# Eight late steps moved from behind the last slots to among them, and the late additions gathered

## The chip, the cores and the metric

The kernel runs on one core of a Trainium2 chip. The metric is the device time of one execution in microseconds; before the change the median of three runs is 490.42 us (490.4 to 490.5). Engines are named as the profile names them: PE is TensorE (PEld its weight loads), DVE VectorE, ACT ScalarE, POOL GpSimd, SP the engine that only issues DMAs.

## The reference

8192 tokens of width 128 (16 sequences of 512) go through two blocks in float32. The first is an RWKV-like layer: a layer norm, four projections, a scan along the sequence, an output projection, a channel mix. The second is a mixture of experts: each token goes to the best of 16 experts, and every token also passes a shared expert.

```python
logits = hidden @ router_w.T
top_vals, top_idx = jax.lax.top_k(logits, K)          # K = 1, N = 16
routed_in = hidden[None, :, :] * scores.T[:, :, None]
gate, up = jnp.split(jnp.einsum('nth,nhf->ntf', routed_in, gate_up_proj), 2, axis=-1)
routed_out = jnp.einsum('ntf,nfh->nth', up * jax.nn.silu(gate), down_proj)
shared = jax.nn.silu(hidden @ shared_gate_w.T) * (hidden @ shared_up_w.T) @ shared_down_w.T
return (shared + routed_out.sum(axis=0)).reshape(b, s, h)
```

Each token's row of the output is its input of this block, plus its one expert's product, plus the shared expert's.

## The kernel before

The kernel has three stages, written out by hand: each engine has a program of its own, and semaphores tie them.

**Rounds** (up to about 345 us of the trace) work on 16 tiles of 512 tokens: the first block, the router, and a part of the shared expert. Each round scatters its tokens' rows, sorted by expert, into a table in DRAM (sorted_rows).

**Slots** (about 355 to 487 us): 79 slots of 128 sorted rows of one expert each, worked on as 40 pairs, the last of one slot. The tensor program's one_turn (line 800) for turn m transposes two pairs of slots in every even turn (L806), then runs the late steps that late_steps(m) names, then the down product of pair m-3 (L815), then the gate and up products of pair m-1 (L822, L823). ScalarE copies the expert's weights (L1076) and takes the silu (L1084), VectorE copies the transposes (L1439), multiplies (L1450) and adds the pair's product to its rows (L1442), GpSimd scatters the rows to the output (L1610), two scatters a pair. SP loads slots ahead into a ring of 12 pairs, and a load into a place of the ring waits for the scatter of the pair that held it.

**Late units** are halves of tiles (256 tokens) whose shared expert doesn't run in the rounds. LATE names 16; the first three run at the end of the rounds, units 3 to 15 stand as late steps. A unit has four: steps 0 and 1 are each the gate and the up product of half of its inner width (unit_product, L427, eight matmul records), with a silu on ScalarE (L853) and a product on VectorE (L1418) behind them; steps 2 and 3 are the two down products (unit_down_late, L435, eight records), and behind step 3 ScalarE copies the sum to SBUF (L856). late_order (line 245) gives the order: (u,0), (u-1,2), (u,1), (u-1,3) for u = 4 to 15, with (15,2), (15,3) at the end. late_steps (line 259) spreads them: one in each of turns 0 and 1, the last LATE_AFTER of them behind the last pair of slots (one in turn 40, two in turn 41, the rest in turn 42), and the others evenly over turns 4 to 39. Inside the slots a late step stands ahead of the turn's slot work on TensorE, from turn 40 on behind it.

late_bank (line 252) gives the PSUM banks of a unit's gate and up products: banks 2 and 3, and for the first halves of units from TWO_PAIRS on banks 4 and 6, which the slots use too. With one pair of banks, a gate product waits for the silu of the half before, an up product for its product on VectorE (lines 469 to 482).

**The end.** When all scatters have landed, SP and GpSimd load the late rows of the output back (load_late, L339): six loads of two units each on SP, two on GpSimd. VectorE adds the shared expert's sum to each unit (add_late, L1430, and L1426 for unit 15), and SP (units 0 to 11) and ScalarE (12 to 15) store them (store_late, L345), each store behind its addition. ADDED_BEHIND says behind which late step's product on VectorE the additions of which units stand; the last two units follow at the very end. VectorE runs its program in order, so an addition holds back all that is written behind it.

Of the kernel before, what the change touches and what calls it, by code (L numbers as in the profile page):

```python
# [53 lines left out]
N_LATE = len(LATE)  # L54
# [39 lines left out]
def program(nc, x, w_main, w_exp, vecs, out):  # L94
# [4 lines left out]
    with ExitStack() as ctx:  # L99
# [12 lines left out]
        def wait(eng, name, t, k=None):  # L112

            of = WHO.get(name, range(NT))
            count = sum(1 for u in of if u <= t)
            if count:
                eng.wait_ge(s[name], (count - 1) * PER[name] + (PER[name] if k is None or t not in of else k))
# [104 lines left out]
        TAB_ROWS = 15  # L222
        ACT_STORES = 4
        SP_LOADS, GP_LOADS = [0, 2, 4, 6, 8, 14], [10, 12]
        ADDED_BEHIND = {(N_LATE - 2, 1): range(0, 4), (N_LATE - 1, 0): range(4, 8), (N_LATE - 1, 1): range(8, N_LATE - 2)}
        HALF_TILE = 5
        EARLY_STATS = 3
        WARM_FIRST, WARM_BEFORE, WARM_BEHIND = 16, (8, 12), 4
        FULL_SLOTS = NTOK // P - NE
        FILL_PAIRS = range(4, 4 + NE)  # L230
        FIRST_LATE = len(C_TILES)
        TWO_PAIRS = N_LATE - 3
        STEPS_BEFORE, LATE_TURN, LATE_AFTER = 1, 4, 16
        GU_BEHIND, DN_BEHIND = 1, 3
        W_BEHIND = GU_BEHIND - 1
        TURNS = NP + DN_BEHIND
# [15 lines left out]
        def late_bank(u, step):  # L252

            n = 2 * (u - FIRST_LATE) + step
            if u >= TWO_PAIRS and step == 0:
                return bank[4], bank[6]
# [152 lines left out]
        def _(pe):  # L409
# [14 lines left out]
            def unit_product(dst, name, pair_, src, half):  # L424

                for j in range(2):
                    ins = mm(dst[:, j * HALF:(j + 1) * HALF], W(name, 2 * pair_ + j), src[:, half * HALF:(half + 1) * HALF],  # L427
                             start=True, stop=True)
                return ins
# [32 lines left out]
            def late_step(u, step):  # L462
                tile, half = LATE[u]
                if step < 2:
                    g_bank, u_bank = late_bank(u, step)
                    if (u, step) in ((FIRST_LATE, 1), (FIRST_LATE + 1, 0)):
                        wait(pe, f"csg{step}", NT)
                        wait(pe, f"cac{step}", NT)
                    if FIRST_LATE < u < TWO_PAIRS:
                        wait(pe, "lsg", u - 1, 2)  # L470
                        if step:
                            wait(pe, "lsg", u, 1)
                    elif u > TWO_PAIRS or u == TWO_PAIRS and step:
                        wait(pe, "lsg", u - 1, step + 1)
                    unit_product(g_bank, "gate", step, hT[tile], half).then_inc(s["lG"], 1)
                    if FIRST_LATE < u < TWO_PAIRS:
                        wait(pe, "lac", u - 1, 2)
                        if step:
                            wait(pe, "lac", u, 1)
                    elif u > TWO_PAIRS or u == TWO_PAIRS and step:  # L480
                        wait(pe, "lac", u - 1, step + 1)
# [613 lines left out]
        def _(dve):  # L1095
# [314 lines left out]
            def late_step(u, step):  # L1410
                if step < 2:
                    wait(dve, "lsg", u, step + 1)
                    wait(dve, "lU", u, step + 1)
                    wait(dve, "lD", u - 2, step + 1)
                    if u < FIRST_LATE + 2:
                        wait(dve, f"cD{step}", NT)
                        wait(dve, f"hD{step}", NT)
                    v.tensor_tensor(late_act(u)[step][:, :], late_sg(u)[step][:, :], late_bank(u, step)[1][:, :], ALU.mult).then_inc(s["lac"], 1)  # L1418

            def add_late(units):  # L1420
                for u in units:
                    if u % 2 == 0:
                        dve.wait_ge(s[tl_sem(u)[0]], tl_sem(u)[1] + 16)
                    if u == N_LATE - 1:
                        wait(dve, "lD", u)
                        v.tensor_tensor(tl_of(u), tl_of(u), late_sum(u)[:, 0:HALF], ALU.add).then_inc(s["tl_add"], 1)  # L1426
                    else:
                        wait(dve, "cbase", NT)
                        wait(dve, "lsh", u)
                        v.tensor_tensor(tl_of(u), tl_of(u), sh_of(u), ALU.add).then_inc(s["tl_add"], 1)  # L1430
# [4 lines left out]
            def one_turn(m):  # L1435
# [15 lines left out]
                if m >= NP:  # L1451
                    for u, step in late_steps(m):
                        late_step(u, step)
                        add_late(ADDED_BEHIND.get((u, step), ()))

# [200 lines left out]
```

## Time and profile before

| what | value |
|---|---|
| median of three runs without a profiler | 490.42 us (490.4 to 490.5) |
| span of the profiled execution, first to last instruction | 510.8 us |
| PE busy, whole span | 485.5 us (95%) |
| DVE, ACT, POOL busy | 368.8 (72%), 320.9 (63%), 353.3 us (69%) |
| mean granted clock of TensorE | 0.997 |
| DMA | 39.33 MB, mean 77 GB/s |

The profiled execution is 20.4 us longer than the median of the others; the page gives its span and no other time for it. Times in rows count from its first instruction. A PE record's end is modelled, so that consecutive matmuls overlap in the rows: the time of a group of them is best read from the start of its first to the start of the next group. In a row of the timeline the text in square brackets is the engine's idle time ahead of it and what ended it; "remote" and "issue" mean that the profile shows no releaser.

### The profile page before, as it was taken

Reading aid. Unit: us, or ns where it says so; the run is one execution under the profiler, and the core shown is the slowest. Engines: PE = TensorE matmul, PEld = TensorE weight load, DVE = VectorE, ACT = ScalarE, POOL = GpSimd, SP = SyncE. Lnnn points to the kernel's source line nnn. Section 1 sums busy time; section 2 is a strip of 40 time slices with the busy share of each in tenths; the row PEclk is TensorE's granted clock in tenths of the full one; section 3 lists DMA queues with packets and bytes.
Section 4 is the critical chain, followed back from the end, with each engine's and each line's share of the span. In section 5 each row is a group of like instructions: output and inputs, shape, how many; then the busy total and the mean of one; then the engine's idle time right before and its main releaser. Section 6 shows DMA issues by size and latency. Waiting matters only on the chain.

```text
span 510.8 us, 10511 instructions
## 1 busy us (share of the span) xinstructions
PE 485.5 (95%) x3093; PEld 391.8 (77%) x3093; DVE 368.8 (72%) x1056; ACT 320.9 (63%) x623; POOL 353.3 (69%) x573
## 2 busy tenths in 40 slices
PE   8899999999999999999999999989999899899777
PEld 6665777777777777868678678778998788779766
DVE  6979999999999999978999896473443443344415
ACT  3576897897897887876879865533544453345212
POOL 6656599889889889876888776762365566556650
PEclk9999999999999999999999999999999999999989
DMA  6015010110110101101011011114886444440027
GB/s 227 3 39 230 21 37 28 62 33 32 62 32 33 62 22 43 62 21 44 22 42 43 1 42 43 43 41 126 205 221 169 125 122 124 125 115 20 23 80 251
DMA packets 33031, 39.33 MB, mean 77 GB/s; under 512 B 4913, under 2 KB 29113, under 8 KB 32720
## 3 DMA queue, kind: packets, MB, share of 16 engines
q1 hardware_dynamic: 26640, 24.98, 16.8%
q0 software_dynamic: 5760, 13.16, 7.4%
q8 instruction: 26, 0.43, 0.4%
q10 hardware_dynamic: 576, 0.52, 0.3%
q14 instruction: 29, 0.24, 0.2%
HBM read 21.69 MB, written 17.93 MB: 78 GB/s over the span
## 4 chain that ended last, share of the span: by engine, by line
PE 76%; DVE 7%; issue 6%; ACT 3%; another core or an unknown queue 3%; POOL 2%; DMA 2%; SPq 0%; DVEq 0%; ACTq 0%; POOLq 0%
PE bank L427 17%; PE bank L420 9%; PE bank L444 6%; PE bank L414 4%; PE bank L435 4%; PE bank L815 3%; PE bank L823 3%; PE bank L822 3%; PE bank L528 3%; PE bank L514 3%; PE bank L540 3%; PE bank L519 3%; PE bank L524 3%; PE bank L688 2%
## 5 line engine op out<-in xcount | busy, mean ns | idle before, releaser
L427 PE MATMUL bank<-hT,wm 128*128 128x256 f32 x512 | 125.9, 385 | 3.3 <-issue 2.7
L427 PEld LDWEIGHTS bank<-hT,wm 128*128 128x128 f32 x512 | 92.6, 192 | 22.2 <-issue 12.1
L1610 POOL DMA_INDIRECT out<-shared x55 | 53.9, 979 | 52.1 <-DVE shared L1442 25.6
L1528 POOL DMA_INDIRECT sorted_rows<-rows,posi x64 | 72.3, 1130 | 19.7 <-issue 16.9
L420 PEld LDWEIGHTS bank<-wm,k 128*128 128x128 f32 x512 | 61.7, 192 | 7.6 <-issue 6.6
L420 PE MATMUL bank<-wm,k 128*128 128x128 f32 x512 | 62.1, 276 | 0.0
L1084 ACT ACTIVATE er<-bank 128x256 f32<-128x256 f32 x40 | 15.3, 383 | 47.5 <-remote 24.3
L1442 DVE TENSOR_TENSOR shared<-bank,shared 128x256 f32<-128x256 f32 x28 | 11.8, 420 | 32.4 <-remote 17.4
L1610 POOL DMA_INDIRECT out<-rows x24 | 23.5, 978 | 14.5 <-issue 8.0
L444 PE MATMUL bank<-wm,actA 128*128 128x128 f32 x240 | 32.9, 281 | 0.0
L944 ACT ACTIVATE h<-rows,smE 128x128 f32<-128x128 f32 x64 | 26.3, 482 | 8.9 <-POOL smE L1504 8.9
L1450 DVE TENSOR_TENSOR e<-er,bank 128x256 f32<-128x256 f32 x40 | 16.7, 418 | 19.7 <-ACT er L1084 9.7
L444 PEld LDWEIGHTS bank<-wm,actA 128*128 128x128 f32 x240 | 29.1, 192 | 0.2 <-issue 0.2
L1574 POOL TENSOR_SCALAR shared<-shared,smA 128x128 f32<-128x128 f32 x64 | 27.6, 442 | 0.0
L965 ACT ACTIVATE xn1tok<-shared,smA 128x128 f32<-128x128 f32 x61 | 25.0, 482 | 2.8 <-POOL smA L1544 2.8
L1514 POOL TENSOR_SCALAR rows<-h,sc 128x128 f32<-128x128 f32 x64 | 25.4, 412 | 1.6
L1552 POOL TENSOR_TENSOR smA<-smA,half 128x8 f32<-128x8 f32 x15 | 25.3, 1684 | 1.3
L888 ACT ACTIVATE xn2T<-bank,vec 128x512 f32<-128x512 f32 x16 | 12.4, 778 | 18.4 <-PE bank L414 17.2
L528 PEld LDWEIGHTS bank<-wm,xn2T 128*128 128x128 f32 x128 | 16.8, 192 | 7.6 <-issue 7.5
L1519 POOL TENSOR_TENSOR xa<-shared,a 128x512 f32<-128x512 f32 x16 | 20.4, 1275 | 0.0
L1329 DVE TENSOR_TENSOR_SCAN den<-decay,e 128x512 f32<-128x512 f32 x16 | 19.4, 1211 | 0.7 <-ACT e L1010 0.7
L1418 DVE TENSOR_TENSOR actB<-sgB,bank 128x512 f32<-128x512 f32 x14 | 9.6, 685 | 14.2 <-ACT sgB L853 7.0
(256 smaller groups left out, 1308.0 us busy)
## 6 DMA issues: line engine op xcount, KB each, us to landing
shared<-sorted_rows SPq DMA_DIRECT2D x56, 128.5 KB
shared<-x SPq DMA_DIRECT2D x16, 256.0 KB
rows<-sorted_rows SPq DMA_DIRECT2D x24, 128.5 KB
wexp<-w_exp SPq DMA_DIRECT2D x2, 1536.0 KB, 8.2
sorted_rows<-filler SPq DMA_DIRECT2D x17, 128.5 KB
shared<-out SPq DMA_DIRECT2D x6, 256.0 KB
out<-shared SPq DMA_DIRECT2D x12, 128.0 KB, 2.2
sorted_rows<-rows,posi POOLq DMA_INDIRECT x64
```

The lines of the kernel that those rows point to most:

```text
L414: ins = nc.tensor.transpose(grp(dst, g), grp(src, g), ident[:, :])
L420: ins = mm(grp(acc, g), grp(lhs, g), W(name, f), start=(f == 0 and g == 0), stop=(f == F // P - 1), skip_group_check=True)
L427: ins = mm(dst[:, j * HALF:(j + 1) * HALF], W(name, 2 * pair_ + j), src[:, half * HALF:(half + 1) * HALF], start=True, stop=True)
L444: ins = mm(grp(acc, 2 * half + g), lhs[:, at_:at_ + P], W("down", 2 * pair_ + j), start=(pair_ == 0 and j == 0 and g == 0), stop=(pair_ == ...
L528: ins = mm(grp(REC_B, g), grp(xn2T[t % 2], g), W("Wrec"), start=True, stop=True)
L944: ins = af(grp(h[t % 2], g), base_of(t)[:, g, :], ACT.Identity, bias=smE[t % 3][:, 3, g:g + 1], scale=smE[t % 3][:, 1, g:g + 1])
L965: ins = af(grp(xn1tok[t % 2], g), grp(xin[t % XR], g), ACT.Identity, bias=smA[t % 3][:, 5, g:g + 1], scale=smA[t % 3][:, 4, g:g + 1])
L1514: ins = g_.tensor_scalar(rows[t % 3][:, g, 0:D], grp(h[t % 2], g), sc[t % 2][:, g:g + 1], 1.0, ALU.mult, ALU.mult)
L1528: g_.indirect_dma_start(sorted_ap, bass.IndirectOffsetOnAxis(posi[t % 3][:, g:g + 1].bitcast(U32), 0), rows[t % 3][:, g, :], None).then_in ...
L1552: g_.tensor_tensor(sm[:, 3:5, :], sm[:, 1:3, :], half8[:, :, :], ALU.pow).then_inc(s["pA"], 1)
L1574: ins = g_.tensor_scalar(grp(xn0[t % 4], g), grp(xin[t % XR], g), smA[t % 3][:, 0, g:g + 1], smA[t % 3][:, 3, g:g + 1], ALU.add, ALU.mult)
L1610: g_.indirect_dma_start(out, bass.IndirectOffsetOnAxis(xr[k % RING][:, j, D:D + 1].bitcast(U32), 0), xr[k % RING][:, j, D + 1:ROW], None, ...
```

## The change

Three numbers of the schedule change. LATE_AFTER goes from 16 to 8: of the 51 late steps that late_steps places, 8 instead of 16 stand behind the last slots, and 41 instead of 33 are spread over turns 4 to 39. TWO_PAIRS goes from 13 to 15: only unit 15 uses banks 4 and 6. ADDED_BEHIND puts the additions of units 0 to 13 all behind the last product on VectorE, (15,1), where they stood in three parts behind (14,1), (15,0) and (15,1). The last two additions stay at the end.

```diff
--- before.py
+++ after.py
@@ -222,15 +222,15 @@
         TAB_ROWS = 15
         ACT_STORES = 4
         SP_LOADS, GP_LOADS = [0, 2, 4, 6, 8, 14], [10, 12]
-        ADDED_BEHIND = {(N_LATE - 2, 1): range(0, 4), (N_LATE - 1, 0): range(4, 8), (N_LATE - 1, 1): range(8, N_LATE - 2)}
+        ADDED_BEHIND = {(N_LATE - 1, 1): range(0, N_LATE - 2)}
         HALF_TILE = 5
         EARLY_STATS = 3
         WARM_FIRST, WARM_BEFORE, WARM_BEHIND = 16, (8, 12), 4
         FULL_SLOTS = NTOK // P - NE
         FILL_PAIRS = range(4, 4 + NE)
         FIRST_LATE = len(C_TILES)
-        TWO_PAIRS = N_LATE - 3
-        STEPS_BEFORE, LATE_TURN, LATE_AFTER = 1, 4, 16
+        TWO_PAIRS = N_LATE - 1
+        STEPS_BEFORE, LATE_TURN, LATE_AFTER = 1, 4, 8
         GU_BEHIND, DN_BEHIND = 1, 3
         W_BEHIND = GU_BEHIND - 1
         TURNS = NP + DN_BEHIND
```

TensorE in the slots, turn 4, the first of five turns (4, 11, 18, 25, 32) that now have two late steps. hT and wm are the late units' inputs and the weights, actB one of their products, an, e and num are slots' weights, products and inputs; a row of the order is an instruction of the program, and "x4" four alike:

```order
 L806 MATMUL bank<-ident,shared 128x128 x4
 L435 MATMUL bank<-wm,actB 128x128 x4
+L427 MATMUL bank<-hT,wm 128x256 x4
 L815 MATMUL bank<-an,e 128x128 x2
 L822 MATMUL bank<-num,an 128x128
```

A gate-and-up step has come in behind the down step that stood there.

TensorE at the very end, from the last slot's down product (L815, one instruction pair for its single slot) on, as it stands before:

```order
L815 MATMUL bank<-rv,e 128x128
L435 MATMUL bank<-wm,den 128x128 x4
L427 MATMUL bank<-hT,wm 128x256 x4
L435 MATMUL bank<-wm,den 128x128 x4
L427 MATMUL bank<-hT,wm 128x256 x4
L435 MATMUL bank<-wm,actB 128x128 x4
L427 MATMUL bank<-hT,wm 128x256 x4
L435 MATMUL bank<-wm,actB 128x128 x4
L427 MATMUL bank<-hT,wm 128x256 x4
L435 MATMUL bank<-wm,den 128x128 x4
L427 MATMUL bank<-hT,wm 128x256 x4
L435 MATMUL bank<-wm,den 128x128 x4
```

(one group, the last two down steps, follows), and as it stands after, to its end:

```order
L815 MATMUL bank<-rv,e 128x128
L435 MATMUL bank<-wm,den 128x128 x4
L427 MATMUL bank<-hT,wm 128x256 x4
L435 MATMUL bank<-wm,den 128x128 x4
L435 MATMUL bank<-wm,actB 128x128 x8
```

Thirteen late steps stood behind the last slot's down product, five do now; three stand between it and the last gate and up products of the slots, as before.

VectorE at the very end after the change, from the product of (14,1) on (L1442 adds the last two pairs of slots to their rows):

```order
L1418 TENSOR_TENSOR den<-ev,bank 128x512
L1442 TENSOR_TENSOR shared<-bank,shared 128x2x128
L1418 TENSOR_TENSOR actB<-sgB,bank 128x512
L1442 TENSOR_TENSOR shared<-bank,shared 128x2x128
L1418 TENSOR_TENSOR actB<-sgB,bank 128x512
L1430 TENSOR_TENSOR shared<-shared,xn1tok 128x256 x4
L1430 TENSOR_TENSOR shared<-shared,xn1T 128x256 x4
L1430 TENSOR_TENSOR shared<-shared,ew 128x256 x4
L1430 TENSOR_TENSOR shared<-shared,kr 128x256 x3
L1426 TENSOR_TENSOR shared<-shared,bank 128x256
```

The additions (L1430) of units 0 to 14 stand in one row; before, four stood behind each of the products (14,1) and (15,0) and the rest behind (15,1).

On POOL and SP the order is the same before and after.

## Rows read from the trace of the kernel before

**Rows 1.** Busy time by stretch: stretch and us, then busy (instructions) per engine, clock, DMA.
```profile
60.00:80.00 20.00, 20.00 (x124) 14.92 (x123) 19.38 (x59) 16.34 (x30) 16.84 (x31) 1.00 0.12 40
356.00:376.00 20.00, 20.00 (x149) 18.79 (x148) 8.42 (x17) 10.64 (x26) 7.86 (x8) 1.00 0.85 219
376.00:480.00 104.00, 93.61 (x670) 86.06 (x668) 43.19 (x94) 45.79 (x115) 60.67 (x62) 1.00 0.41 114
```

**Rows 2.** Timeline of the tail, all engines: start us, us, engine, line, operation, tiles.
```profile
486.49 0.39 PE L815 MATMUL bank<-rv,e 128*128 128x128 f32 x2
...
487.65 1.89 PE L427 MATMUL bank<-hT,wm 128*128 128x256 f32 x8
...
489.58 0.42 DVE L1442 TENSOR_TENSOR shared<-bank,shared 128x256 f32<-128x256 f32 x1
...
491.15 0.98 POOL L1610 DMA_INDIRECT out<-shared  x1 [0.30 <-issue]
493.38 3.15 SPq L339 DMA_DIRECT2D shared<-out  x6
...
493.95 0.60 ACT L853 ACTIVATE sgB<-bank 128x512 f32<-128x512 f32 x1 [6.65 <-remote]
494.44 0.38 ACT L856 ACTIVATE kr<-bank 128x256 f32<-128x256 f32 x1
494.57 0.69 DVE L1418 TENSOR_TENSOR actB<-sgB,bank 128x512 f32<-128x512 f32 x1 [4.57 <-ACT sgB L853]
...
494.96 2.05 PE L435 MATMUL bank<-wm,actB 128*128 128x128 f32 x8 [2.76 <-ACT kr L856]
...
505.32 1.42 DVE L1430 TENSOR_TENSOR shared<-shared,ew 128x256 f32<-128x256 f32 x4
505.39 2.05 PE L435 MATMUL bank<-wm,actB 128*128 128x128 f32 x16
```

**Rows 3.** Timeline early in the slots, all engines.
```profile
355.60 0.44 PE L806 MATMUL bank<-ident,shared 128*128 128x128 f32 x2 [0.39 <-DMA shared<-sorted_rows]
...
363.15 0.60 PE L806 MATMUL bank<-ident,shared 128*128 128x128 f32 x4
...
363.59 1.11 PE L435 MATMUL bank<-wm,actB 128*128 128x128 f32 x8
...
364.54 0.61 PE L815 MATMUL bank<-an,e 128*128 128x128 f32 x4
...
364.98 0.39 PE L822 MATMUL bank<-num,th 128*128 128x128 f32 x2
...
365.18 0.42 DVE L1442 TENSOR_TENSOR shared<-bank,shared 128x256 f32<-128x256 f32 x1 [0.39 <-issue]
...
365.88 1.89 PE L427 MATMUL bank<-hT,wm 128*128 128x256 f32 x8
...
367.60 0.61 PE L815 MATMUL bank<-xn2T,e 128*128 128x128 f32 x4
```

**Rows 4.** DMA issues of the tail: tiles, queue, count, KB each, us to landing.
```profile
shared<-out SPq DMA_DIRECT2D x6, 256.0 KB
out<-shared SPq DMA_DIRECT2D x12, 128.0 KB, 2.2
shared<-out POOLq DMA_DIRECT2D x2, 256.0 KB, 6.3
out<-shared ACTq DMA_DIRECT2D x4, 128.0 KB, 1.9
```

**Rows 5.** Busy time by stretch, in the tail.
```profile
494.00:495.00 1.00, 0.04 (x1) 0.07 (x1) 0.42 (x1) 1.00 (x3) 1.00 (x2) 0.80 0.30 68
495.00:500.00 5.00, 5.00 (x24) 4.64 (x25) 1.56 (x4) 0.91 (x2) 0.48 (x1) 0.70 0.93 313
508.00:509.00 1.00, 0.00 (x0) 0.00 (x0) 0.08 (x1) 0.00 (x0) 0.00 (x0) 1.00 1.05 365
509.00:510.00 1.00, 0.00 (x0) 0.00 (x0) 0.00 (x0) 0.00 (x0) 0.00 (x0) 1.00 0.86 297
```

## The prediction

> **What bounds the kernel now.** I read the busy shares by stretch first. In the long stage of rounds TensorE has no gap: 20.00 of 20 us busy between 60 and 80 us. The slot stage begins the same way, 20.00 of 20 us from 356 to 376 us, and then gets holes: 93.61 of 104 us from 376 to 480 us, 10.4 us idle, with ScalarE and VectorE under half busy [rows 1]. So the question for this change is what those holes are. The timeline of the tail answers half of it: TensorE's last up product of unit 13 stands at about 489.4 us, but ScalarE, idle for 6.65 us, starts the silu that reads the gate product before it only at 493.95 us, put down to no known releaser [rows 2]. Between 376 and 494 us others learn of products later than the records of these products end. The profiled execution is also 20.4 us longer than the runs without a profiler (span 510.8 us against a median of 490.42 us).
>
> Next, a sum from the early, gapless rows [rows 3]: a gate-and-up step of a late unit takes 365.88 to 367.60 = 1.72 us, a down step 363.59 to 364.54 = 0.95 us, and a slot pair 0.44 (down) + 0.90 (gate, up) + 0.22 (its half of the 0.44 of transposes) = 1.56 us. From the first transpose of the stage (355.60 us, where its first slots had landed) to the end TensorE has 39.5 pairs, 25 gate-and-up steps and 26 down steps: 61.6 + 43.0 + 24.7 = 129.3 us. The trace spends 355.60 to 507.44 = 151.8 us on them, 22.5 us more [rows 2, 3]. That excess is nearly the 20.4 us that the timed runs don't have. I conclude that in a timed run the slot stage and the tail are TensorE without holes, give or take 2 us, and that from the last down step to the end of the span only 510.8 - 507.44 = 3.4 us follow.
>
> **What the change moves.** LATE_AFTER goes from 16 to 8. Steps (12,1), (11,3), (13,0), (12,2), (13,1), (12,3), (14,0), (13,2), four of each kind, leave the tail and are spread over the slots: 4 x 1.72 + 4 x 0.95 = 10.7 us of TensorE. The loop carries 41 steps instead of 33 over 36 turns, so five turns get two and none is left without. With them go four silus (0.60 us) and two copies (0.38) on ScalarE, 3.2 us, and four products (0.69) on VectorE, 2.8 us; both engines have more than half of the stage free [rows 1], so they cost nothing [durations: rows 2]; with that cover gone they would cost some 3 us. No DMA changes its place on a queue; but everything that hangs on the last slot comes later by what the loop grows.
>
> TWO_PAIRS 13 to 15: the first halves of units 13 and 14 no longer take banks 4 and 6, which slots use, but banks 2 and 3. There a gate product waits for the silu and the product of the half before, 1.3 us, and between the two lie at least a down step or a slot pair's 1.34 us: nothing; uncovered, up to 5.2 us for the four halves.
>
> **What becomes the end.** Call t0 the start of the last slot's down product, 486.49 us in the trace [rows 2]. Behind it hangs a second chain that TensorE's tail covers today: VectorE adds the last slot (489.58), GpSimd scatters it (491.15), SP sees all stores landed and issues the loads of the late rows (493.38), the loads land, VectorE adds, the stores go out [rows 2]. The first link was late in the trace, 3.1 us from the down product's start; early in the stage VectorE's addition starts 0.64 us after the down product starts (365.18 against 364.54) [rows 3]. The other two are 493.38 - 489.58 = 3.80 us. So t0 to the loads is 4.2 to 6.9 us (0.39 for the last, single slot, 0.03, 3.80; or 493.38 - 486.49). The loads are 8 x 256 KB, the stores 16 x 128 KB [rows 4], 4.19 MB together on the same DMA engines. They moved 313 GB/s where they were densest over 5 us, 365 in the best us [rows 5]: 13.4 us, or 11.5. With 0.9 us until the first bytes and 1.0 after the last [rows 5] that is 15.3 us; the bounds are 13.4 and the 17.4 that the trace shows from the first load to the end (493.38 to 510.8), where TensorE held the additions back. I take 15.3. The chain is then 19.5 us from t0, or 22.2 with the trace's late link.
>
> The Trainium skill, Perfetto Trace Analysis, section Engine Utilization, puts a single core's 16 DMA engines at about 435 GB/s; by it 4.19 MB would take 9.6 us, an estimate, and the chain would be 3.8 us shorter, the change +4 us instead of the forecast. The rows of the tail stay at 365 GB/s and below, so I stay with them [rows 5].
>
> In the kernel before TensorE has 5 x 1.72 + 8 x 0.95 + 0.22 = 16.4 us behind t0, and 3.4 to the end: 19.8 us; in the trace 24.3, with 2.76 us of waiting for a copy and some 1.5 us lost to a granted clock of 0.70 on average from 495 to 500 us [rows 2, 5]. The two ends are thus level today: 19.8 against 19.5, or 24.3 against 22.2. In the changed kernel TensorE has only 5.5 us behind t0 (2 x 0.95, 0.95, 1.72, 0.95), but the chain keeps its length, and t0 comes up to 10.7 us later.
>
> The additions: they now wait for the last product step, some 4 us after t0 (0.22 + 0.95 + 1.72, then the product's 0.69 and a start), when the first load is only just issued, 4.2 us after t0. So moving them costs nothing; 14 x 0.36 us (four in 1.42) [rows 2] run as loads land, inside the 15.3.
>
> **The sum.** 10.7 + 22.2 - 24.3 = +8.6 us by the trace's own latenesses, 10.7 + 19.5 - 19.8 = +10.4 without. From this goes what the loop's holes take up. The profile alone allows 0 to 10.4; the timed runs leave about 2; I take 1.3 off the middle, 9.5: +8.2 us. Against the profiled execution that is 510.8 + 8.2 = 519.0 us of span; against the median of the timed runs 490.42 + 8.2 = 498.6 us.
>
> **Rivals.** (a) The holes are real, and the loop swallows all eight steps: t0 stays, and the end is the chain's, 22.2 against 24.3, -2.1 us: 488.3 us. It holds if a timed run has at least 10 us of idle TensorE in the loop. For it: the 10.4 us of rows 1. Against: no hole from 356 to 376 us at the same load, and the 20.4 us that timed runs are shorter. The Trainium skill, Perfetto Trace Analysis, section Identifying the Most-Contended Engine, speaks for this rival: matmul busy time is a poor measure, the share of weight loads the better one. By it the loop has 104 - 86.06 = 17.9 us of room; but the gapless stretch from 60 to 80 us shows 14.92 of 20 us of weight loads, so here that share does not say that an instruction more is free.
> (b) Half is swallowed, 5.3 us: +3.3 to +5.1, about 494 us. For it: a slot pair needs answers from ScalarE and VectorE within a turn, and three turns without a step (15, 27, 39) last only 1.56 us today, less than two scatters of 0.98 + 0.30 us each on GpSimd [rows 2]. Against: the same rows as under (a).
> (c) The loop suffers beyond the work put in: in the five turns with two steps, or in units 13 and 14, the wait for silu and product shows, 1 us a turn: +5, 503.6 us. Against: gate-and-up and down steps alternate, so the same banks don't follow at once.
> (d) The change doesn't shift the end, by a part swallowed of 9 us: 490.4 us.
>
> **Numbers.** Forecast, 496 to 502 us: 0.60. (b) 0.17, (a) 0.10, (c) 0.10, (d) 0.03. 0.2% of the time is 1.0 us, about what timing can tell from no change. Faster is (a), 0.10; same is (d) with a thin slice of (b), 0.04; slower the rest, 0.86. The range from 492.5 to 502.5 us leaves out (a), (d), the low end of (b) and most of (c), 0.2 together.
>
> **What would show it.** Right: TensorE's last record some 10 us or more before the span's end, where it was 3.4; the loads of the late rows issued some 8 to 10 us later than 493.4 in the profile; all fourteen additions waiting for loads, with DMA at 270 to 350 GB/s from the first load to the last store. Each gap between turns in the loop shrinking, with the loop no longer than before, would show (a) or (b). Wrong: loads issued where they were; or the stretch from the first load to the end well under 13 us, which would make the chain too long in my sum.

## The result, and the profile after

The changed kernel takes 500.8 us (median of four, 500.14 to 501.16), the kernel before 490.41 (490.39 to 490.5): the ratio is 1.0206 (95% interval 1.0193 to 1.0218), 10.4 us slower. The forecast was 498.6 us. Each run also lists its span, and its time is that span and 2.0 us around it (500.14 against 498.1). On that footing the first profiled execution of the kernel before, with its span of 510.8 us, was not 20.4 but 22.4 us longer than the median, close to the excess of 22.5 us that the prediction found in it.

Busy time by stretch of the changed kernel, to be read beside [rows 1, 5] (stretch and us, busy time and instructions of PE, PEld, DVE, ACT and POOL, granted clock, DMA share, GB/s):

```profile
356.00:376.00 20.00, 20.00 (x151) 19.04 (x150) 9.73 (x20) 11.37 (x27) 9.14 (x10) 1.00 0.87 215
376.00:480.00 104.00, 104.00 (x777) 99.97 (x776) 49.59 (x103) 52.91 (x125) 67.26 (x70) 1.00 0.40 111
485.00:490.00 5.00, 0.00 (x0) 0.00 (x0) 1.36 (x4) 0.00 (x0) 0.00 (x0) 0.77 0.86 255
490.00:493.00 3.00, 0.00 (x0) 0.00 (x0) 2.90 (x9) 0.00 (x0) 0.00 (x0) 0.50 1.06 369
```

The slot stage is TensorE without any hole, 104.00 of 104 us, where [rows 1] have 93.61. From 485 us on TensorE does nothing, and the DMA moves 255 to 369 GB/s.

The tail in its timeline, all engines, to be read beside [rows 2]; the first row is from the start of the slots (start us, us, engine, line, operation, tiles):

```profile
353.51 0.44 PE L806 MATMUL bank<-ident,shared 128*128 128x128 f32 x2
...
477.12 0.39 PE L815 MATMUL bank<-rv,e 128*128 128x128 f32 x2
...
477.99 0.42 DVE L1442 TENSOR_TENSOR shared<-bank,shared 128x256 f32<-128x256 f32 x1
...
479.92 0.98 POOL L1610 DMA_INDIRECT out<-shared  x1 [0.30 <-issue]
...
480.95 2.05 PE L435 MATMUL bank<-wm,actB 128*128 128x128 f32 x16
...
482.14 3.16 SPq L339 DMA_DIRECT2D shared<-out  x6
...
484.93 1.43 DVE L1430 TENSOR_TENSOR shared<-shared,xn1tok 128x256 f32<-128x256 f32 x4 [3.97 <-DMA shared<-out]
...
490.10 1.43 DVE L1430 TENSOR_TENSOR shared<-shared,xn1T 128x256 f32<-128x256 f32 x4 [3.74 <-DMA shared<-out]
...
493.31 1.92 ACTq L345 DMA_DIRECT2D out<-shared  x4
493.86 0.42 DVE L1426 TENSOR_TENSOR shared<-shared,bank 128x256 f32<-128x256 f32 x1
```

The last slot's down product starts at 477.12. VectorE has added the slot at 478.41, GpSimd scatters it at 479.92, SP issues the loads at 482.14. TensorE's last record ends at 483.00. VectorE then waits 3.97 us for the first load and 3.74 us for the third, adds all units with no late step's product between them, and the four stores on ScalarE start at 493.31. The span ends at 498.1, 15.1 us behind TensorE's last record; in [rows 2] that was 3.4 us.

### The profile page after: what moved, and what is told of

The parts are those of the page before. It is cut to its first block, busy times and chain, and to the rows that moved or that the text cites. A ratio compares the mean times of both kernels' runs of the same rounds, so it can differ in the third digit from the quotient of the medians.

```text
span 498.1 us, 10515 instructions
## 1 busy us (share of the span) xinstructions
PE 476.7 (96%) x3093; PEld 388.4 (78%) x3093; DVE 370.8 (74%) x1056; ACT 323.5 (65%) x623; POOL 352.9 (71%) x573
## 4 chain that ended last, share of the span: by engine, by line
PE 80%; DVE 5%; DMA 4%; issue 4%; POOL 4%; ACT 2%; SPq 1%; POOLq 0%; DVEq 0%; ACTq 0%
PE bank L427 19%; PE bank L420 9%; PE bank L444 6%; PE bank L435 4%; PE bank L414 4%; PE bank L822 4%; PE bank L823 4%; PE bank L815 4%; PE bank L528 3%; PE bank L514 3%; PE bank L540 3%; PE bank L524 3%; PE bank L519 3%; PE bank L688 2%; PE bank L697 2%
## 5 line engine op out<-in xcount | busy, mean ns | idle before, releaser
L1084 ACT ACTIVATE er<-bank 128x256 f32<-128x256 f32 x40 | 15.3, 383 | 48.7 <-PE bank L823 48.6
L1442 DVE TENSOR_TENSOR shared<-bank,shared 128x256 f32<-128x256 f32 x28 | 11.9, 424 | 25.1 <-PE bank L815 25.1
L1519 POOL TENSOR_TENSOR xa<-shared,a 128x512 f32<-128x512 f32 x16 | 20.4, 1276 | 0.0
L1329 DVE TENSOR_TENSOR_SCAN den<-decay,e 128x512 f32<-128x512 f32 x16 | 19.5, 1218 | 0.7 <-ACT e L1010 0.7
L435 PE MATMUL bank<-wm,den 128*128 128x128 f32 x144 | 19.4, 281 | 0.0
```

The costliest lines, as they stand in the source:

```text
L435: ins = mm(grp(acc, g), lhs[:, j * HALF + g:(j + 1) * HALF:2], W("down", 2 * pair_ + j), start=(pair_ == 0 and j == 0 and g == 0), stop=(p ...
```

## The experiments

**The kernel before, once more.** No edit; a second profile, since the first has holes that the first trace of the changed kernel has not.

> The kernel before, unchanged, for a second profile. Theory (one work list: TensorE is gapless from the first slot to its last product, and the holes of the first profile belong to that one execution): no holes in the slot stage, TensorE 20.0 of 20 us busy in every stretch from 360 to 460 us, last TensorE record near 483 us as in the changed kernel (483.0), span near 488 us. Rival (the holes are real, and the added steps filled them): again some 10 us idle from 376 to 480 us, and a span near 511 us.

It took 490.86 us, with a span of 488.8 us. Busy time by stretch of this second profile:

```profile
355.00:376.00 21.00, 21.00 (x159) 19.83 (x158) 10.62 (x22) 11.81 (x28) 9.79 (x10) 1.00 0.87 224
376.00:480.00 104.00, 104.00 (x772) 99.77 (x772) 51.00 (x108) 53.23 (x126) 69.07 (x72) 1.00 0.44 125
```

No hole: 104.00 of 104 us. And its tail, with a row from the start of the slots ahead of it:

```profile
354.09 0.44 PE L806 MATMUL bank<-ident,shared 128*128 128x128 f32 x2 [0.69 <-DMA shared<-sorted_rows]
...
467.02 0.39 PE L815 MATMUL bank<-rv,e 128*128 128x128 f32 x2
...
467.88 0.42 DVE L1442 TENSOR_TENSOR shared<-bank,shared 128x256 f32<-128x256 f32 x1
...
470.76 0.98 POOL L1610 DMA_INDIRECT out<-shared  x1 [0.30 <-issue]
...
472.98 3.93 SPq L339 DMA_DIRECT2D shared<-out  x6
...
478.21 0.76 DVE L1430 TENSOR_TENSOR shared<-shared,xn1tok 128x256 f32<-128x256 f32 x2 [1.36 <-DMA shared<-out]
...
480.62 0.76 DVE L1430 TENSOR_TENSOR shared<-shared,xn1T 128x256 f32<-128x256 f32 x2 [0.38 <-DMA shared<-out]
...
481.50 2.05 PE L435 MATMUL bank<-wm,actB 128*128 128x128 f32 x16
...
482.18 1.43 DVE L1430 TENSOR_TENSOR shared<-shared,ew 128x256 f32<-128x256 f32 x4 [0.20 <-DMA shared<-out]
...
483.98 1.90 ACTq L345 DMA_DIRECT2D out<-shared  x4
484.54 0.41 DVE L1426 TENSOR_TENSOR shared<-shared,bank 128x256 f32<-128x256 f32 x1
```

So the 10.4 us of holes and the long silences in [rows 1, 2] belong to that one execution, whose span was 22.0 us longer than this one's. This row set is the one to compare with: t0 at 467.02 (477.12 after, 10.1 us later), TensorE's end at 483.55 (483.00 after), the loads at 472.98, the end at 488.8. The starts of the two executions differ a little: here TensorE waits 0.69 us for the rows of the second pair of slots (354.09), in the changed kernel it transposes them at 353.51. Counted from these transposes, t0 comes at 112.93 us before and 123.61 after, 10.7 us later. Behind TensorE's end there are 5.3 us here, not 3.4: VectorE waits for loads three times (1.36 us at 478.21, 0.38 at 480.62, 0.20 at 482.18), and the first of the last four stores starts only at 483.98.

**More and fewer steps behind the slots.** Two kernels with 20 and with 12 late steps there, additions as before (with 12, units 14 and 15, with 20, units 12 to 15 have their first halves on banks 4 and 6).

```diff
-        TWO_PAIRS = N_LATE - 3
-        STEPS_BEFORE, LATE_TURN, LATE_AFTER = 1, 4, 16
+        TWO_PAIRS = N_LATE - 4      # with 12: N_LATE - 2
+        STEPS_BEFORE, LATE_TURN, LATE_AFTER = 1, 4, 20      # or 12
```

> 20 late steps behind the last slots instead of 16 (the first halves of units from 12 on banks 4 and 6), additions as before. Theory: the end is the later of TensorE's last product + 3.4 us and of the last slot's down product (t0) + 21.0 us, the chain that the changed kernel's profile shows (477.12 to 498.1). t0 comes 5.3 us earlier, so TensorE alone sets the end: 483.0 + 3.4 + 2.7 us outside the span = 489.1 us, 1.3 us faster than before. Rival (the loop's holes take steps for nothing): the loop stays as long, the tail grows by 5.3 us: 495.7 us.

> 12 late steps behind the last slots (first halves of units 14 and 15 on banks 4 and 6), additions in three parts as before. Theory: t0 comes 5.3 us later than before and the chain of 21.0 us behind it sets the end: 495.5 us, half of the way to the changed kernel. Rival (the loop swallows part, or the loss comes from the additions that stand behind the last product): 490 to 492.5 us.

With 20: 489.09 us, ratio to before 0.9965 (0.9951 to 0.9979). With 12: 495.41 us, ratio 1.0101 (1.0082 to 1.0119). Both fit the theory, and neither a loop that swallows steps. The timeline of the tail with 20:

```profile
462.01 0.38 PE L815 MATMUL bank<-rv,e 128*128 128x128 f32 x2
...
469.62 3.15 SPq L339 DMA_DIRECT2D shared<-out  x6
...
476.42 1.42 DVE L1430 TENSOR_TENSOR shared<-shared,xn1tok 128x256 f32<-128x256 f32 x4
...
481.81 2.05 PE L435 MATMUL bank<-wm,actB 128*128 128x128 f32 x16
...
483.53 1.90 ACTq L345 DMA_DIRECT2D out<-shared  x4
```

TensorE ends at 483.86, the span at 487.2, 3.3 us later, and no addition waits for a load: here TensorE does set the end. The loads start 7.6 us behind t0 instead of 6.0 with 16 steps, since GpSimd's scatters lag behind the shorter loop, and it costs nothing. That the expected sum meets the measured time to the tenth is partly luck: it counts 2.7 us outside the span, where the runs' own spans give 2.0, and puts TensorE's end at 483.0 instead of 483.86. With 12:

```profile
471.70 0.38 PE L815 MATMUL bank<-rv,e 128*128 128x128 f32 x2
...
476.74 3.16 SPq L339 DMA_DIRECT2D shared<-out  x6
...
479.54 1.43 DVE L1430 TENSOR_TENSOR shared<-shared,xn1tok 128x256 f32<-128x256 f32 x4 [4.00 <-DMA shared<-out]
...
483.99 1.62 DVE L1430 TENSOR_TENSOR shared<-shared,xn1T 128x256 f32<-128x256 f32 x4 [2.42 <-DMA shared<-out]
...
486.26 2.07 PE L435 MATMUL bank<-wm,actB 128*128 128x128 f32 x8 [3.43 <-DVE actB L1418]
```

The loads start 5.04 us behind t0 and the span ends at 492.1, 20.4 us behind t0, as after the change (21.0). TensorE itself waits 3.43 us for VectorE, which sits in additions whose loads have not landed (2.42 us at 483.99): the kernel with 12 is bound by the loads.

**The additions alone.** 16 steps as before, the additions of units 0 to 13 all behind the last product.

```diff
-        ADDED_BEHIND = {(N_LATE - 2, 1): range(0, 4), (N_LATE - 1, 0): range(4, 8), (N_LATE - 1, 1): range(8, N_LATE - 2)}
+        ADDED_BEHIND = {(N_LATE - 1, 1): range(0, N_LATE - 2)}
```

> 16 late steps behind the last slots as before, and only the additions moved: all of units 0 to 13 behind the last product. Theory: here that product is late (about 14 us behind t0), loads have landed by then, and fourteen additions and their stores run behind it: some 2 us slower, 492.4 us. The prediction's claim that the move costs nothing holds only where the product comes before the loads. Rival (the additions are free wherever they stand): 490.4 us.

492.27 us, ratio 1.0035 (1.0022 to 1.0048), 1.7 us. Timeline of its tail:

```profile
467.22 0.38 PE L815 MATMUL bank<-rv,e 128*128 128x128 f32 x2
...
473.19 4.24 SPq L339 DMA_DIRECT2D shared<-out  x6
...
481.02 0.69 DVE L1418 TENSOR_TENSOR actB<-sgB,bank 128x512 f32<-128x512 f32 x1 [1.98 <-PE bank L427]
...
481.62 1.42 DVE L1430 TENSOR_TENSOR shared<-shared,xn1tok 128x256 f32<-128x256 f32 x4
...
482.06 5.85 SPq L345 DMA_DIRECT2D out<-shared  x12
```

The product of (15,1) comes at 481.02, 13.8 us behind t0, when loads issued at 473.19 have landed; fourteen additions and the first store wait for it. In the changed kernel that product comes at 480.27, before the loads are even issued, and the same edit has nothing to hold back. So the move costs 1.7 us with 16 steps; that it is free with 8 is read from that order, and no run has 8 steps with the additions in three parts. By the kernel's text none could: with 8 steps the products of (14,1) and (15,0) stand in turns 40 and 41, ahead of VectorE's addition of the last slot in turn 42. An addition behind one of them would wait for a load, the load for the scatter of the last slot, and that scatter for an addition that VectorE reaches only afterwards. TWO_PAIRS follows in the same way: with 8 steps the first halves of units 13 and 14 stand inside the loop, where the slots' own products and transposes use banks 4 and 6 (XGU_B, XT6_B) and no wait keeps the two apart. The change is thus one decision, LATE_AFTER, and two edits that it forces.

**The banks alone.** 16 steps, additions as before, TWO_PAIRS at 15.

```diff
-        TWO_PAIRS = N_LATE - 3
+        TWO_PAIRS = N_LATE - 1
```

> The kernel before with TWO_PAIRS at 15 alone: the first halves of units 13 and 14 use banks 2 and 3 behind the slots. Theory: a down step of 0.95 us lies between two halves; the silu ends 1.7 us and the product 2.7 us after a half's start, the next half's gate starts 2.67 us and its up product 3.5 us after it, so no wait shows: 490.4 us. Rival (the shared banks cost a wait of some 0.5 to 1 us in each of four halves): 492 to 494 us.

Ratio 1.0012 (1.0003 to 1.0021; medians 491.57 and 491.07 us on that chip): 0.1%, at most 0.2% or 1 us. Its TensorE rows show no wait between halves; the one gap stands ahead of the very last down step:

```profile
480.97 1.43 DVE L1430 TENSOR_TENSOR shared<-shared,xn1T 128x256 f32<-128x256 f32 x4 [2.56 <-DMA shared<-out]
481.06 1.10 PE L435 MATMUL bank<-wm,actB 128*128 128x128 f32 x8
...
483.05 1.21 PE L435 MATMUL bank<-wm,actB 128*128 128x128 f32 x8 [0.89 <-DVE actB L1418]
```

It waits 0.89 us for VectorE's last product, which stands behind additions in VectorE's program, and these waited 2.56 us for a load; it does not wait for a bank. Whether the 0.1% comes from there, these runs don't tell.

**The loads taken out.** The changed kernel without loads of the late rows.

```diff
-            all_stored(sp)
-            load_late(sp, SP_LOADS)
...
-                    if u % 2 == 0:
-                        dve.wait_ge(s[tl_sem(u)[0]], tl_sem(u)[1] + 16)
+                    if u == 0:
+                        all_stored(dve)
...
-                        v.tensor_tensor(tl_of(u), tl_of(u), sh_of(u), ALU.add).then_inc(s["tl_add"], 1)
+                        v.tensor_copy(tl_of(u), sh_of(u)).then_inc(s["tl_add"], 1)
...
```

> The changed kernel without the eight loads of the late rows (2.1 MB); VectorE copies the shared sums instead of adding them to the loaded rows, behind the landing of all scatters, so the late rows of the output lack all but the shared expert. Theory: in the changed kernel the chain behind the last slot sets the end, and the loads are the largest part of it; without them copies (0.36 us each) and stores (0.5 us each on SP) start right at 482.2 us, the last store lands at about 490.7 us: 493.4 us, 7.4 us less than the changed kernel's 500.8. Rival (additions in one block and their stores set the end, the loads hide): 499 to 501 us.

493.96 us, ratio to before 1.0056 (1.004 to 1.0071), against 1.0206 with loads: 1.5%, 7.4 us. Timeline of its tail (this kernel is two lines shorter there, so L813 is the product that is L815 elsewhere, L1608 the scatter, L1428 the copy in place of the addition):

```profile
478.28 0.39 PE L813 MATMUL bank<-rv,e 128*128 128x128 f32 x2
...
481.09 0.98 POOL L1608 DMA_INDIRECT out<-shared  x1 [0.30 <-issue]
...
483.46 0.90 DVE L1428 COPY shared<-xn1tok 128x256 f32<-128x256 f32 x4 [1.34 <-DMA out<-shared]
483.78 6.06 SPq L345 DMA_DIRECT2D out<-shared  x12
...
486.20 1.90 ACTq L345 DMA_DIRECT2D out<-shared  x4
```

VectorE starts 2.4 us behind the last scatter and never waits again; the last four stores start 5.1 us behind the last scatter, where the changed kernel needs 13.4 (479.92 to 493.31). From t0 (478.28) to the end of the span (492.4) it is 14.1 us, against 21.0 with loads: the loads are 6.9 us of the chain, a third of it; I had expected them to be its largest part. Some 5.0 us stand ahead of them, from t0 to their issue, and about 9 behind, additions and stores. That part doesn't depend on copies being shorter than additions (0.90 us against 1.43 for four): from the first copy to the end it is 8.9 us here (483.46 to 492.4), and 9.0 from the first addition to the end in the run with the additions alone (481.62 to 490.6), where all loads had landed.

**Spread additions, and 24 steps.** With 20 steps the end is TensorE's, and behind it only additions and four stores are left, so I moved additions ahead; and with 24 steps I looked whether the slope goes on.

```diff
-        ADDED_BEHIND = {(N_LATE - 2, 1): range(0, 4), (N_LATE - 1, 0): range(4, 8), (N_LATE - 1, 1): range(8, N_LATE - 2)}
+        ADDED_BEHIND = {(N_LATE - 2, 0): range(0, 2), (N_LATE - 2, 1): range(2, 4), (N_LATE - 1, 0): range(4, 10), (N_LATE - 1, 1): range(10, N_LATE - 2)}
-        TWO_PAIRS = N_LATE - 3
-        STEPS_BEFORE, LATE_TURN, LATE_AFTER = 1, 4, 16
+        TWO_PAIRS = N_LATE - 4
+        STEPS_BEFORE, LATE_TURN, LATE_AFTER = 1, 4, 20
```

With 24 steps LATE_AFTER is 24 and TWO_PAIRS N_LATE - 5, the additions as before at first.

> 20 late steps behind the last slots, and the additions earlier: units 0 and 1 behind (14,0), 2 and 3 behind (14,1), 4 to 9 behind (15,0), 10 to 13 behind (15,1). Theory: with 20 the end is TensorE's last product and what follows it, and of that the four stores on ScalarE begin up to 1 us earlier: 488.5 us, 0.6 us less than with 20 alone (489.1). Rival (only the last addition and its store count): 489.1 us. A load that has not landed when its addition is due would hold VectorE and so TensorE: 490 us or more.

> 24 late steps behind the last slots, additions as before. Theory: TensorE sets the end already with 20, its work is the same whatever stands where: 489.1 us, as with 20. Rival (each step moved behind the slots gains): 488 us or less, on the slope between 16 and 20.

20 with spread additions: 488.32 us, ratio 0.994 (0.9927 to 0.9954). 24: 488.98 us, ratio 0.996 (0.9944 to 0.9975), the same as 20: the slope ends where TensorE sets the end. A last group put 20, 20 with spread additions and 24 with spread additions on one chip:

> 20 late steps behind the last slots, additions as before, once more, beside the spread additions on one chip. Theory: 0.35% faster than before, as in its first run; the difference to the spread version, 0.2%, comes from the additions alone.

> 20 late steps and the additions spread (2, 2, 6 and 4 units behind the last four products), once more, beside 20 alone. Theory: 0.15 to 0.25% faster than 20 alone, since the four last stores start sooner; ratio to before 0.994. Rival (its first ratio of 0.994 was that chip's): the same as 20 alone, 0.9965.

> 24 late steps behind the last slots, additions 2, 2, 4, 4 and 2 units behind the last five products. Theory: TensorE's end is the same as with 20; only two additions are left for the last product, so the last stores start another 0.7 us sooner: ratio to before 0.993. Rival (only unit 15's addition and store count behind TensorE's end, they don't move): 0.994 to 0.996.

Ratios to before: 20 again 0.996 (0.9945 to 0.9975), spread again 0.9946 (0.9931 to 0.9961), 24 spread 0.9952 (0.9937 to 0.9968). The version with 20 steps and spread additions, 488.2 us, is faster than both kernels. Beside 20 alone it was ahead both times, by 0.25 and by 0.14%. The intervals to the kernel before overlap, but on the one chip its six runs lie at 487.66 to 488.44 us and those of 20 alone at 488.39 to 489.43, so it is probably the faster one, by less than 1 us. In the second group's profile its last stores did start sooner:

```profile
473.53 0.75 DVE L1430 TENSOR_TENSOR shared<-shared,xn1tok 128x256 f32<-128x256 f32 x2
...
481.59 2.05 PE L435 MATMUL bank<-wm,actB 128*128 128x128 f32 x16
...
482.63 1.94 ACTq L345 DMA_DIRECT2D out<-shared  x4
483.67 0.42 DVE L1426 TENSOR_TENSOR shared<-shared,bank 128x256 f32<-128x256 f32 x1 [0.40 <-PE bank L435]
```

They start 1.01 us ahead of TensorE's end (481.59 + 2.05), with 20 alone 0.33 us ahead. In the profile of its first run, the slowest of five, they start only 0.41 us ahead, and one addition waits 0.55 us for its load. With 24 spread:

```profile
456.05 0.38 PE L815 MATMUL bank<-rv,e 128*128 128x128 f32 x2
...
465.22 3.15 SPq L339 DMA_DIRECT2D shared<-out  x6
...
481.17 2.05 PE L435 MATMUL bank<-wm,actB 128*128 128x128 f32 x16
...
481.55 2.50 ACTq L345 DMA_DIRECT2D out<-shared  x4
483.26 0.42 DVE L1426 TENSOR_TENSOR shared<-shared,bank 128x256 f32<-128x256 f32 x1 [0.94 <-PE bank L435]
```

they start earlier still, 1.67 us ahead of that end, and nothing more is gained: the addition of unit 15 at 483.26 waits for TensorE and its store follows, as the rival had it.

## Why the prediction was right, step by step

- **What bounds the slots: right.** TensorE is gapless in both kernels (104.00 of 104 us). From t0 to TensorE's end it has 16.53 us before (467.02 to 483.55) and 5.88 after (477.12 to 483.00): 10.65 us have moved ahead of t0, forecast 10.7 (the forecast's 5.5 us for what stays behind t0 leaves out the last slot's own 0.22). From the first landed slots to its end TensorE takes 129.5 us in the second profile (354.09 to 483.55), where the sum from early rows gave 129.3. Eight steps in already full turns cost their full price.
- **The reason given for the holes: half right.** I concluded that a timed run has none, and that holds. But I set the timed runs apart as runs without a profiler. Their spans lie 2.0 us under their times, and a profiled execution as long as they are (490.86 us) has no holes; the first profile was simply a longer execution. What delayed its signals stays open: no run repeated it.
- **Swallowed, 1.3 us: wrong, the term should be 0.** Nothing is swallowed. With it left out, the sum's two ends are 8.6 and 10.4 us, and the one without the trace's late links was the right one to use. That is the 2.2 us by which the forecast is short. But that this end meets the measured 10.4 us to the tenth is luck, as the next two points show.
- **The chain behind t0: right in kind, 1.5 us short.** t0 to the loads 5.0 us (4.2 to 6.9 forecast): VectorE's addition comes 0.87 us behind t0, forecast 0.42, and GpSimd's last scatter, paced by the one before it, starts 1.93 us behind the addition's start instead of 1.57. Loads to the end 16.0 us (15.3, bounds 13.4 and 17.4). Together 21.0 us, against 19.5.
- **The end before: the wrong one taken, and 2 us short.** I took TensorE's end and 3.4 us, 19.8 us behind t0. The second profile has 21.8. The two ends were not level: with 16 steps the loads and stores already were the later one, which is why 20 steps are faster: VectorE's waits for loads add up to 1.9 us, as much as the end lies further behind TensorE's (5.3 against 3.3 us). The two errors nearly cancel: 10.1 + 21.0 - 21.8 = 9.3 us between the two spans, and the medians differ by 10.4. The 1.1 us between these is the choice of executions: the one profiled after is the fastest of its four (500.14, 0.7 us under the median), the second one before took 0.4 us more than the median (490.86).
- **The page's rate of DMA: the rows were right.** By the 435 GB/s of the Trainium skill (Perfetto Trace Analysis, section Engine Utilization) the change would have cost 4 us, by the prediction's estimate; the densest stretch after moves 369 GB/s over 3 us, and from 485 to 490 us, where the third load is waited for, only 255.
- **The additions and the banks: right in effect.** The additions have nothing to hold back in the changed kernel, but cost 1.7 us where the last product is late; the banks cost 0.1%, at most 0.2%. The prediction treats both edits as choices; by the kernel's text LATE_AFTER at 8 forces them.
- **Rivals.** (a) and (b) fall with the second profile and with the runs of 12 and 20 steps: 12 steps are half way to 8 (5.1 of 10.4 us), and with 20 the tail grows by four steps and the time doesn't, so the loop became shorter by them. (d) falls with the result. The Trainium skill's rule on weight loads (Perfetto Trace Analysis, section Identifying the Most-Contended Engine) gave 17.9 us of room; in the second profile weight loads are busy 99.77 of 104 us, so the room too was that one execution's, all but 4.2 us. (c) falls: the stage with its five turns of two steps shows no hole, and t0 moved by no more than the work put in.

## What to carry to other kernels

Work put behind a loop to cover a chain of transfers costs nothing as long as that chain is the later end; moved into the loop it delays the chain by its full length, if the loop's engine is full. Find both ends from the same starting point, here the last slot's product, and put as much behind it as makes them level: here the time falls from 8 over 12 and 16 to 20 steps and then stays. Before holes in a profile are taken for room, compare that execution's length with the other runs', span with span.

## What was not expected of the hardware

One execution of an unchanged kernel can have a span of 510.8 us, in which ScalarE sits idle for 6.65 us and starts a silu 4.4 us after the records of its unit's products have ended (489.54 to 493.95), where a second has 488.8 us and no such holes. And the more work leaves the slots, the more the scatters lag: the loads start 5.0, 5.0, 6.0, 7.6 and 9.2 us behind t0 with 8, 12, 16, 20 and 24 steps behind the slots (477.12 to 482.14, 471.70 to 476.74, 467.02 to 472.98, 462.01 to 469.62, 456.05 to 465.22 us with 24 spread). By the rows GpSimd needs 2 x 1.28 us a pair, and a turn of TensorE only 1.56 us without a late step and 2.51 with a down step; this reason is worked out, no run tests it alone.
